# Front state and residual sum turned in 32x32 blocks by VectorE through a DRAM scratch

## The chip, the cores and the metric

One core of one Trainium2 chip. The time is that of the device, in microseconds, from the start to the end of one execution; lower is better. The kernel before takes 1272.34 us, the median of 3 runs (1271.83 to 1272.41).

## What is computed

`x` is 32 graphs of 256 nodes with 256 features, `adj` a sparse 256x256 matrix shared by all. Four layers, each `x = layernorm(x + L(x))`:

```python
# L0: gated graph network, three steps
a = concat(adj @ h, adj @ h)
z = sigmoid(a @ w3.T + h @ u3.T + b);  r = sigmoid(a @ w4.T + h @ u3.T + b)
hv = tanh(a @ w5.T + (r * h) @ u5.T + b);  h = (1 - z) * h + z * hv
# L1: attention without softmax
rel = adj.T * (q @ k.T);  rel = rel / norm(rel, axis=2);  out = rel @ v
# L2: (adj @ x) @ weight + bias
# L3: (D^-1/2 adj D^-1/2) @ (x @ weight) + bias
```

## The kernel before

Everything is fp32. A product is made of three TensorE products of fp32r parts: each operand is split into `hi` (a ScalarE copy that rounds) and `lo` (VectorE: the value minus `hi`). So every tensor that enters a product passes ScalarE and VectorE once. TensorE's products all go through `product` (L430).

Graphs are taken in pairs (16 pairs; two graphs are 512 columns). There are two lanes with their own PSUM banks `ps0` and `ps1`: `front` does steps 1 and 2 of the gated network for pair p, `back` does step 3 for pair q = p - 1 and then, as `main`, the attention and the two convolutions of that pair. One call of `body(p, q)` does all of this; it is written once for each engine as a list in program order, and it runs 14 times (once alone, then 13 times in a `Fori` loop). `finish` does the last pairs in its own order. Semaphores alone order the engines; each engine keeps its list's order, so an operation that waits holds up all behind it on its engine.

One step of a lane is `mix` (adj times h), `base`, `reset`, `update`, `candidate_mixed`, `candidate_reset` on TensorE, each twice (k = 0, 1), with `a_hi`, `reset_gate`, `rh_hi`, `update_gate`, `candidate` on ScalarE and `a_lo`, `reset_h`, `rh_lo`, `keep`, `candidate_part` and the new state (`first_h`, `hand_over_h`) on VectorE. The state is held with features on partitions (`feat`); `mix` of the next step needs it with nodes on partitions (`node_hi`, `node_lo`). `turn_h` (L529) makes that with 4 TensorE transposes a graph into `front.ps1`, from which ScalarE and VectorE make `node_hi` and `node_lo`.

`new_sum` makes the residual sum `sum_t`, again with features on partitions. `turn_sum` (L533) turns it with 4 transposes a graph into `back.ps1`, and from there VectorE takes the statistics (`stats_of`, L1251) and the normalised value (`normalise`, L1267). The products `keys`, `relate` and `values` work on the raw sum, with centred weights; so the relation has to be scaled by 1 / variance, and `mask` (L1307) multiplies by it and by adj in one operation for each half. `values` writes the bank in which the turned sum lay, so it waits for `normalise`. GpSimd makes `rstd` (L362, L364), `inv_var` and `std`; `relation_squares` (L907) scales by `std`.

The input of a pair comes twice: `x_front` in rows, and `x_blocks` in an order in which 32x32 block transposes on VectorE (`turn_blocks`, L1233) give the turned input. SP's queue, in a pass: `load_front`, `load_blocks` (four transfers), `keep_input` (a copy of the turned input for the residual), `store`.

## Time and profile before

| | |
|---|---|
| median of 3 runs | 1272.34 us |
| the profiled execution | 1271.8 us |
| its span, first to last instruction | 1270.0 us |
| TensorE busy | 1240.6 us (98%) |
| VectorE busy | 1031.4 us (81%) |
| ScalarE busy | 583.7 us (46%) |
| GpSimd busy | 192.4 us (15%) |
| mean granted TensorE clock | 0.995 of full |

The profile gives each engine's instructions with start and duration. Busy time is what instructions cover; for TensorE the shown ends of neighbours overlap, so the distance from start to start tells what one costs. An instruction's line is often that of a helper (all products have L430), and the names on it (`f_ps<-hf_feat_hi,u3T_hi`) tell which it is: `f_` is the front lane, `b_` the back lane, `hf_` and `hb_` their states. In lines after "idle before" a releaser is named when the engine stood still.

### The profile page before, as it was taken

What the parts mean: (1) busy time and instruction counts of PE and PEld (TensorE: products, weight loads), DVE (VectorE), ACT (ScalarE), POOL (GpSimd) and SP (SyncE); (2) the same over time, 40 slices, a digit from 0 to 9 for tenths busy, and PEclk for the clock granted to TensorE, in tenths of its full rate; (3) what the DMA queues carried; (4) which work ended last, traced back from release to release, by engine and by line L of the source; (5) the groups of instructions that cost most, each with busy time, mean ns of one, the idle gap of its engine ahead of it and who ended that gap; (6) DMA issues with size and microseconds to landing.
All of it is one profiled execution on the core that took longest, in us unless ns stands there. A gap on an engine that the chain in (4) does not pass through costs nothing.

```text
span 1270.0 us, 21112 instructions
## 1 busy us (share of the span) xinstructions
PE 1240.6 (98%) x7664; PEld 1103.3 (87%) x7664; DVE 1031.4 (81%) x2274; ACT 583.7 (46%) x1007; POOL 192.4 (15%) x366
## 2 busy tenths in 40 slices
PE   7799999999999999999999999999999999999996
PEld 6589899898988989899898988989889898998895
DVE  5668889788888878888788888878888788895898
ACT  4444444444444444454444444444454445444442
POOL 0001112020210202112020110202112021110023
PEclk9999999999999999999999999999999999999999
DMA  7020110202001020010202002020010202000000
GB/s 199 1 50 1 38 30 1 66 0 59 7 17 50 0 66 0 33 33 0 66 0 50 17 17 50 0 66 0 21 45 0 66 0 49 17 17 18 1 1 34
DMA packets 86168, 37.56 MB, mean 30 GB/s; under 512 B 64768, under 2 KB 83200, under 8 KB 86144
## 3 DMA queue, kind: packets, MB, share of 16 engines
q1 hardware_dynamic: 84592, 36.71, 10.6%
q0 software_dynamic: 192, 0.52, 0.2%
q8 instruction: 15, 0.25, 0.1%
q10 hardware_dynamic: 1360, 0.01, 0.1%
q14 instruction: 9, 0.07, 0.0%
HBM read 20.45 MB, written 8.39 MB: 23 GB/s over the span
## 4 chain that ended last, share of the span: by engine, by line
PE 94%; DVE 4%; DMA 1%; POOL 1%; issue 0%; ACT 0%; ACTq 0%; DVEq 0%
PE b_ps L430 46%; PE f_ps L430 43%; PE f_ps L525 2%; PE b_ps L525 1%; DMA bias_in<-in_L_gnn_u_b 1%; PE b_ps L571 1%; DVE f_stats L1251 0%; DVE hf_feat L1267 0%; DVE normed L1267 0%; POOL f_rstd L364 0%; DVE f_cand L1184 0%; DVE b_stats L1251 0%; DVE f_kept L1178 0%; ACTq L827 0%; DVE f_a_lo L1162 0%
## 5 line engine op out<-in xcount | busy, mean ns | idle before, releaser
L362 POOL TENSOR_TENSOR b_var_eps<-b_moments,eps 128x2 f32<-128x2 f32 x120 | 44.1, 368 | 827.6 <-DVE b_moments L1258 827.6
L364 POOL TENSOR_TENSOR b_rstd<-b_var_eps,neg_half 128x2 f32<-128x2 f32 x120 | 97.0, 808 | 9.4
L866 ACT ACTIVATE f_z<-f_ps,bias_z 128x512 f32<-128x512 f32 x66 | 45.2, 685 | 92.5 <-PE f_ps L430 92.5
L870 ACT ACTIVATE f_cand<-f_ps,bias_c 128x512 f32<-128x512 f32 x66 | 45.5, 690 | 85.1 <-PE f_ps L430 85.1
L1168 DVE TENSOR_TENSOR f_gate<-f_gate,hf_feat 128x512 f32<-128x512 f32 x66 | 45.2, 685 | 46.2 <-ACT f_gate L858 46.0
L1251 DVE BATCH_NORM_STATS2 b_stats<-b_ps 128x6 f32<-128x256 f32 x180 | 68.3, 421 | 13.9 <-PE b_ps L430 13.3
L430 PE MATMUL f_ps<-adjT_hi,hf_node_hi 128*128 128x256 f32 x264 | 74.6, 283 | 0.0
L430 PE MATMUL f_ps<-adjT_hi,hf_node_lo 128*128 128x256 f32 x264 | 74.3, 282 | 0.0
L430 PE MATMUL f_ps<-adjT_lo,hf_node_hi 128*128 128x256 f32 x264 | 74.2, 281 | 0.0
L1290 DVE TENSOR_TENSOR b_rh_lo<-b_ps,b_rh_hi 128x512 fp32r<-128x512 f32 x90 | 61.9, 688 | 13.7 <-ACT b_rh_hi L824 13.4
L824 ACT ACTIVATE f_a_hi<-f_ps 128x512 fp32r<-128x512 f32 x66 | 39.0, 593 | 71.8 <-PE f_ps L430 71.8
L824 ACT ACTIVATE b_rh_hi<-b_ps 128x512 fp32r<-128x512 f32 x90 | 53.7, 597 | 34.8 <-PE b_ps L430 32.8
L824 ACT ACTIVATE b_a_hi<-normed 128x512 fp32r<-128x512 f32 x60 | 37.7, 628 | 54.8 <-DVE normed L1267 54.8
L1267 DVE TENSOR_SCALAR normed<-b_ps,b_moments,b_rstd 128x256 f32<-128x256 f32 x120 | 59.3, 536 | 0.3 <-POOL b_rstd L364 0.3
L1162 DVE TENSOR_TENSOR f_a_lo<-f_ps,f_a_hi 128x512 fp32r<-128x512 f32 x66 | 45.2, 686 | 13.8 <-ACT f_a_hi L824 13.6
L1168 DVE TENSOR_TENSOR b_gate<-b_gate,hb_feat 128x512 f32<-128x512 f32 x30 | 20.8, 692 | 43.8 <-ACT b_gate L858 42.6
L858 ACT ACTIVATE f_gate<-f_ps,bias_r 128x512 f32<-128x512 f32 x66 | 45.1, 684 | 24.3 <-PE f_ps L430 24.1
L430 PE MATMUL f_ps<-f_a_hi,w4T_hi 128*128 128x512 f32 x132 | 53.6, 406 | 1.0 <-DVE f_a_lo L1162 1.0
L1184 DVE TENSOR_TENSOR f_cand<-f_z,f_cand 128x512 f32<-128x512 f32 x66 | 45.6, 690 | 9.8 <-ACT f_cand L870 9.8
L430 PE MATMUL f_ps<-f_a_hi,w34T_hi 128*128 128x512 f32 x132 | 53.3, 404 | 0.0
L430 PE MATMUL f_ps<-hf_feat_hi,u3T_hi 128*128 128x512 f32 x132 | 52.5, 398 | 0.3 <-DVE hf_feat_lo L1216 0.3
L372 POOL TENSOR_TENSOR b_norm_inv<-b_norm_sq,neg_half 128x2 f32<-128x2 f32 x30 | 26.0, 866 | 176.4 <-DVE b_norm_sq L1321 176.4
(325 smaller groups left out, 4610.5 us busy)
## 6 DMA issues: line engine op xcount, KB each, us to landing
x_front<-in_x SPq DMA_DIRECT2D x16, 512.0 KB, 3.5
x_blocks<-in_x SPq DMA_DIRECT2D x60, 128.0 KB, 3.4
input_t<-hf_feat SPq DMA_DIRECT2D x15, 512.0 KB, 2.9
out<-result SPq DMA_DIRECT2D x15, 512.0 KB, 3.0
b_cand<-in_L_gnn_u_w SPq DMA_DIRECT2D x2, 256.0 KB, 8.9
bias_out<-in_L_gnn_bias POOLq DMA_DIRECT2D x4, 128.0 KB, 6.3
b_z<-in_L_gnn_w_w SPq DMA_DIRECT2D x1, 512.0 KB, 11.4
b_gate<-in_L_gnn_w_w SPq DMA_DIRECT2D x1, 512.0 KB, 12.4
```

Source lines behind the costliest of these rows:

```text
L364: pool.tensor_tensor(Y.rstd[:, g], Y.var_eps[:, g], neg_half[:], ALU.pow).then_inc(Y.s_rstd, 1)
L430: last = pe.matmul(bank, s, m, start=start and i == 0, stop=stop and i == len(terms) - 1, skip_group_check=True)
L824: return act.activation(dst, src, ACT.Copy)
L858: act.activation(L.gate[:, k], L.ps0[:, k], ACT.Sigmoid, bias=bias_r[:, k:k + 1]).then_inc(L.s_r, 1)
L866: act.activation(L.z[:, k], L.ps0[:, k], ACT.Sigmoid, bias=bias_z[:, k:k + 1]).then_inc(L.s_z, 1)
L870: act.activation(L.cand[:, k], L.ps1[:, k], ACT.Tanh, bias=bias_c[:, k:k + 1]).then_inc(L.s_tanh, 1)
L1162: dve.tensor_tensor(L.a_lo[:, k], L.ps1[:, k], full(L.a_hi[:, k]), ALU.subtract).then_inc(L.s_a_lo, 1)
L1168: dve.tensor_tensor(L.gate[:, k], L.gate[:, k], L.state.feat[:, k], ALU.mult).then_inc(L.s_rh, 1)
L1184: dve.tensor_tensor(L.cand[:, k], L.z[:, k], L.cand[:, k], ALU.mult).then_inc(L.s_zc, 1)
L1251: last = dve.bn_stats(Y.stats[:, g, c], layer_sum(Y, j, g, c))
L1267: last = dve.tensor_scalar(dst[:, g, c], layer_sum(Y, j, g, c), Y.moments[:, g, c, 0:1], Y.rstd[:, g, c:c + 1], ALU.subtract, ALU.mult)
L1290: dve.tensor_tensor(lo[:, g], src, full(hi[:, g]), ALU.subtract).then_inc(done, 1)
```

## The change

In the 14 passes of `body`, the front state after step 1 and the residual sum are no longer turned by TensorE. VectorE transposes 32x32 blocks (`turn_state`, `turn_sum_blocks`, two operations of 128x512 each) into a free SBUF tile, with the four row blocks side by side; SP writes the tile to a DRAM scratch (512 KB) and, when it has landed, reads it back in four transfers of 128 KB, which set the blocks on their final partitions. `moved_hi` and `moved_lo`, `stats_of` and `normalise` read the tile that comes back, in runs of 32 elements. `finish` and the state handed to the back lane keep the TensorE turn.

1 / variance is applied to the values (`values_hi`, `values_lo`) and no more in `mask`, which becomes one operation; `relation_squares` scales by `rstd`, and `std` is gone. `values` waits for `normalise` in `finish` only. The lists of `body` are put in a new order on TensorE, ScalarE, VectorE and GpSimd. The tiles that hold the blocks before and after the trip are tiles of the kernel that are free at the time: `front.gate` and `front.z` for the state, `normed` and `result` for the sum.

```diff
+def scratch(name):
+    return nc.dram_tensor(name, (4, 32, 4, 256), F32).ap()
+
+def quarters(t):
+    return t[:].rearrange("p c (u n) -> p (c u) n", u=2)
+
+state_f.scratch = scratch("turn_f")
+state_f.blocks, state_f.moved = quarters(front.gate), quarters(front.z)
+
...
+main.scratch = scratch("turn_sum")
+main.sum_blocks, main.sum_moved = (t[:].rearrange("p g c d -> p (g c) d") for t in (main.normed, main.result))
...
+    def move_blocks(S, turn):
+
+        sp.wait_ge(S.s_blocks, 2 * turn)
+        sp.dma_start(S.scratch.rearrange("b i a n -> (b i) a n"), S.blocks).then_inc(S.s_written, 16)
+        sp.wait_ge(S.s_written, 16 * turn)
+        for a in range(4):
+            sp.dma_start(S.moved[32 * a:32 * a + 32],
+                         S.scratch[:, :, a].rearrange("b i n -> i b n")).then_inc(S.s_moved, 16)
+
+    def move_sum(Y, q):
+
+        sp.wait_ge(Y.s_sum_blocks, upto(q))
+        sp.dma_start(Y.scratch.rearrange("b i a n -> (b i) a n"), Y.sum_blocks).then_inc(Y.s_sum_written, 16)
+        sp.wait_ge(Y.s_sum_written, 16 * q + 16)
+        for a in range(4):
+            sp.dma_start(Y.sum_moved[32 * a:32 * a + 32],
+                         Y.scratch[:, :, a].rearrange("b i n -> i b n")).then_inc(Y.s_sum_moved, 16)
+
...
         keep_input(p)
+        move_sum(main, p - 1)
+        move_blocks(state_f, p)
         store(main, p - 1)
...
         if j == 0:
             pool.wait_ge(Y.s_rstd, ln(q, 0, g))
             pool.tensor_tensor(Y.inv_var[:, g], Y.rstd[:, g], Y.rstd[:, g], ALU.mult).then_inc(Y.s_inv_var, 1)
-            pool.tensor_tensor(Y.std[:, g], Y.var_eps[:, g], Y.rstd[:, g], ALU.mult).then_inc(Y.s_std, 1)
...
-    def values(Y, q, g):
+    def values(Y, q, g, turned=False):
         pe.wait_ge(Y.s_sum_lo, upto(q))
-        pe.wait_ge(Y.s_normed, ln(q, 0, g))
+        if turned:
+            pe.wait_ge(Y.s_normed, ln(q, 0, g))
...
+    def moved_hi(S, v, g, turn):
+        act.wait_ge(S.s_moved, 64 * turn)
+        if S is state_b and later(v):
+            act.wait_ge(back.s_mixed, upto(v - 1))
+        rows = S.moved[:, :, g * P:(g + 1) * P].rearrange("p q (u i) -> p u q i", i=32)
+        copy(S.node_hi[:, g].rearrange("p h (c q i) -> p (h c) q i", q=4, i=32), rows).then_inc(S.s_node_hi, 1)
+
...
     def values_hi(Y, q, g):
-        graph_hi(Y.v_hi, Y.ps1[:, g], Y.s_v, upto(q, g), g, Y.s_v_hi)
+        act.wait_ge(Y.s_v, upto(q, g))
+        act.wait_ge(Y.s_inv_var, upto(q, g))
+        for c in range(C):
+            last = act.activation(Y.v_hi[:, g, c], Y.ps1[:, g, c * D:(c + 1) * D], ACT.Copy,
+                                  scale=Y.inv_var[:, g, c:c + 1])
+        last.then_inc(Y.s_v_hi, 1)
...
     def relation_squares(Y, q, g):
         act.wait_ge(Y.s_masked, upto(q, g))
-        act.wait_ge(Y.s_std, upto(q, g))
+        act.wait_ge(Y.s_rstd, ln(q, 0, g))
         for c in range(C):
-            last = act.activation(Y.rel_sq[:, g, c], Y.rel[:, g, c], ACT.Square, scale=Y.std[:, g, c:c + 1])
+            last = act.activation(Y.rel_sq[:, g, c], Y.rel[:, g, c], ACT.Square, scale=Y.rstd[:, g, c:c + 1])
         last.then_inc(Y.s_rel_sq, 1)
...
+    def turn_state(S, v, c):
+        dve.wait_ge(S.s_feat, upto(v, c))
+        out = S.blocks.rearrange("p q (u c i) -> p u q c i", c=C, i=32)[:, :, :, c]
+        dve.transpose(out, S.feat[:, c].rearrange("p (u q i) -> p u q i", q=4, i=32)).then_inc(S.s_blocks, 1)
+
+    def moved_lo(S, v, g):
+        dve.wait_ge(S.s_node_hi, upto(v, g))
+        rows = S.moved[:, :, g * P:(g + 1) * P].rearrange("p q (u i) -> p u q i", i=32)
+
+        def cells(t):
+            return t[:, g].rearrange("p h (c q i) -> p (h c) q i", q=4, i=32)
+
+        dve.tensor_tensor(cells(S.node_lo), rows, full(cells(S.node_hi)), ALU.subtract).then_inc(S.s_node_lo, 1)
+
...
+
+    def turn_sum_blocks(Y, q, c):
+        dve.wait_ge(Y.s_sum_t, upto(q, c))
+        if later(q):
+            dve.wait_ge(s_stored, 16 * q)
+        out = Y.sum_blocks.rearrange("p q (u c i) -> p u q c i", c=C, i=32)[:, :, :, c]
+        dve.transpose(out, Y.sum_t[:, c].rearrange("p (u q i) -> p u q i", q=4, i=32)).then_inc(Y.s_sum_blocks, 1)
+
+    def moved_rows(Y, g, c):
+        at = 64 * (C * g + c)
+        return Y.sum_moved[:, :, at:at + 64]

     def layer_sum(Y, j, g, c):
         if j == 1:
             return Y.normed[:, g, c]
...
-    def stats_of(Y, q, j, g):
-        if j == 0:
-            dve.wait_ge(Y.s_sum_turned, upto(q, g))
+    def stats_of(Y, q, j, g, turned=False):
+        if j == 0 and turned:
+            dve.wait_ge(Y.s_sum_turned, g + 1)
+        elif j == 0:
+            dve.wait_ge(Y.s_sum_moved, 64 * q + 64)
...
         for c in range(C):
-            last = dve.bn_stats(Y.stats[:, g, c], layer_sum(Y, j, g, c))
+            src = layer_sum(Y, j, g, c) if j or turned else moved_rows(Y, g, c)
+            last = dve.bn_stats(Y.stats[:, g, c], src)
...
             dve.wait_ge(s_stored, 16 * q)
         for c in range(C):
-            last = dve.tensor_scalar(dst[:, g, c], layer_sum(Y, j, g, c), Y.moments[:, g, c, 0:1],
-                                     Y.rstd[:, g, c:c + 1], ALU.subtract, ALU.mult)
+            src, cells = layer_sum(Y, j, g, c), dst[:, g, c]
+            if j == 0 and not turned:
+                src = moved_rows(Y, g, c).rearrange("p b (h i) -> p h b i", i=32)
+                cells = cells.rearrange("p (h b i) -> p h b i", b=4, i=32)
+            last = dve.tensor_scalar(cells, src, Y.moments[:, g, c, 0:1], Y.rstd[:, g, c:c + 1],
+                                     ALU.subtract, ALU.mult)
         last.then_inc(Y.s_normed, 1)
...
     def values_lo(Y, q, g):
-        graph_lo(Y.v_lo, Y.v_hi, graph_bank(Y.ps1, g), Y.s_v_hi, upto(q, g), g, Y.s_v_lo)
+        dve.wait_ge(Y.s_v_hi, upto(q, g))
+        for c in range(C):
+            last = dve.scalar_tensor_tensor(Y.v_lo[:, g, c], Y.ps1[:, g, c * D:(c + 1) * D],
+                                            Y.inv_var[:, g, c:c + 1], full(Y.v_hi[:, g, c]), ALU.mult,
+                                            ALU.subtract)
+        last.then_inc(Y.s_v_lo, 1)

     def mask(Y, q, g):

         dve.wait_ge(Y.s_rel, upto(q, g))
-        dve.wait_ge(Y.s_inv_var, upto(q, g))
-        for c in range(C):
-            last = dve.scalar_tensor_tensor(Y.rel[:, g, c], Y.ps0[:, g, c * N:(c + 1) * N],
-                                            Y.inv_var[:, g, c:c + 1], adj_nat[:, c], ALU.mult, ALU.mult)
-        last.then_inc(Y.s_masked, 1)
+        dve.tensor_tensor(Y.rel[:, g], graph_bank(Y.ps0, g), adj_nat[:], ALU.mult).then_inc(Y.s_masked, 1)

...
```

TensorE's new list in `body` (P = 2p, N = 2p+1; the last number is k or g):

```
mix(back) 0,1; base(back) 0,1; mix(front,P) 0; reset(back) 0,1; update(back) 0,1; candidate_mixed(back) 0;
candidate_reset(back) 0; candidate_mixed(back) 1; candidate_reset(back) 1; mix(front,P) 1; base(front,P) 0,1;
reset(front,P) 0,1; update(front,P) 0,1; candidate_mixed(front,P) 0; candidate_reset(front,P) 0;
candidate_mixed(front,P) 1; candidate_reset(front,P) 1; keys 0,1; values 0; relate 0; values 1; relate 1;
base(front,N) 0; sum_squares 0; base(front,N) 1; attend 0; mix(front,N) 0,1; sum_squares 1; attend 1;
reset(front,N) 0,1; candidate_mixed(front,N) 0; mix_nodes 0,0; update(front,N) 0; mix_nodes 0,1;
convolve 0,0; convolve 0,1; update(front,N) 1; candidate_reset(front,N) 0; candidate_mixed(front,N) 1;
candidate_reset(front,N) 1; mix_nodes 1,0; mix_nodes 1,1; turn_h(state_b) 0,1; convolve 1,0; convolve 1,1
```

VectorE's new list in `body` (P = 2p, N = 2p+1; the second number is k or g; of `main`'s, j comes before it):

```
input_nodes_lo 0,1; a_lo(back) 0,1; turn_blocks 0; reset_h(back) 0; input_lo 0; reset_h(back) 1; rh_lo(back) 0;
a_lo(front,P) 0; rh_lo(back) 1; keep(back) 0; residual 0; keep(back) 1; turn_blocks 1; candidate_part(back) 0;
input_lo 1; residual 1; new_sum 0; candidate_part(back) 1; turn_sum_blocks 0; new_sum 1; a_lo(front,P) 1;
turn_sum_blocks 1; reset_h(front,P) 0; sum_lo 0; reset_h(front,P) 1; rh_lo(front,P) 0,1; keep(front,P) 0,1;
sum_lo 1; stats_of 0,0; stats_of 0,1; candidate_part(front,P) 0; first_h 0; turn_state 0;
candidate_part(front,P) 1; first_h 1; turn_state 1; moments_of 0,0; keys_lo 0,1; feat_lo(state_f,N) 0;
moments_of 0,1; normalise 0,0; mask 0; normalise 0,1; feat_lo(state_f,N) 1; values_lo 0; mask 1;
squares_sum 0; relation_lo 0; norms 0; values_lo 1; moved_lo 0,1; sum_attended 0; squares_sum 1;
stats_of 1,0; relation_lo 1; moments_of 1,0; a_lo(front,N) 0; norms 1; a_lo(front,N) 1; normalise 1,0;
sum_attended 1; stats_of 1,1; moments_of 1,1; fill 0,0; conv_x_lo 0,0; normalise 1,1; reset_h(front,N) 0;
fill 0,1; conv_x_lo 0,1; conv_ax_lo 0,0; reset_h(front,N) 1; keep(front,N) 0; rh_lo(front,N) 0; conv_ax_lo 0,1;
stats_of 2,0; moments_of 2,0; rh_lo(front,N) 1; stats_of 2,1; normalise 2,0; moments_of 2,1; fill 1,0;
conv_x_lo 1,0; keep(front,N) 1; normalise 2,1; candidate_part(front,N) 0; fill 1,1; hand_over_h 0;
conv_x_lo 1,1; candidate_part(front,N) 1; hand_over_h 1; conv_ax_lo 1,0; (the rest as before)
```

ScalarE's list follows the same order: `input_nodes_hi` first, `update_gate(back)` between the two `rh_hi(back)`, and around the state turn `candidate(front, 2p)` 0,1; `feat_hi` 0; `keys_hi` 0,1; `values_hi` 0; `feat_hi` 1; `relation_squares` 0; `values_hi` 1; `relation_hi` 0; `moved_hi` 0,1; `relation_hi` 1; `relation_squares` 1; `a_hi` 0,1.

## Rows read from the trace of the kernel before

**Rows 1.** The page's part on busy time: share of the span and count of each engine.
```profile
PE 1240.6 (98%) x7664; PEld 1103.3 (87%) x7664; DVE 1031.4 (81%) x2274; ACT 583.7 (46%) x1007; POOL 192.4 (15%) x366
```

**Rows 2.** Windows: start:end and length, each engine's busy us, clock, DMA share, GB/s.
```profile
447.22:523.72 76.50, 76.50 (x479) 68.25 (x478) 63.55 (x140) 35.78 (x62) 11.91 (x22) 1.00 0.10 27
...
70.70:1141.50 1070.80, 1070.80 (x6666) 955.45 (x6665) 890.49 (x1962) 501.44 (x870) 166.80 (x308) 1.00 0.10 27
1190.00:1270.00 80.00, 66.52 (x490) 61.73 (x488) 70.02 (x192) 28.32 (x50) 21.75 (x44) 0.96 0.04 14
```

**Rows 3.** Timeline of TensorE: start, duration, instruction. First matmuls of successive blocks.
```profile
406.63 0.39 PE L430 MATMUL f_ps<-f_a_hi,w5T_hi 128*128 128x512 f32 x1
...
408.03 0.40 PE L430 MATMUL f_ps<-f_rh_hi,u5T_hi 128*128 128x512 f32 x1
...
410.84 0.28 PE L430 MATMUL b_ps<-b_rh_hi,sum_hi 128*128 128x256 f32 x1
```

**Rows 4.** Timeline of TensorE: a state turn, and one graph of the sum turn.
```profile
412.26 1.04 PE L525 MATMUL f_ps<-ident,hf_feat 128*128 128x128 f32 x8
413.05 0.36 PE L430 MATMUL b_ps<-wvT_hi,sum_hi 128*128 128x256 f32 x1
413.25 0.28 PE L430 MATMUL b_ps<-wvT_lo,sum_hi 128*128 128x256 f32 x1
413.37 0.28 PE L430 MATMUL b_ps<-wvT_hi,sum_lo 128*128 128x256 f32 x1
...
471.02 0.60 PE L525 MATMUL b_ps<-ident,b_cand 128*128 128x128 f32 x4
471.38 0.48 PE L430 MATMUL f_ps<-f_a_hi,w4T_hi 128*128 128x512 f32 x1
471.69 0.39 PE L430 MATMUL f_ps<-f_a_lo,w4T_hi 128*128 128x512 f32 x1
```

**Rows 5.** Groups of VectorE: busy us, mean ns of one, idle before.
```profile
L1307 DVE SCALAR_TENSOR_TENSOR b_gate<-b_ps,b_inv_var,adj_nat 128x256 f32<-128x256 f32 x60 | 26.2, 478 | 0.1
L1233 DVE STREAM_TRANSPOSE hf_feat<-x_blocks 128x512 f32<-128x512 f32 x30 | 21.0, 704 | 0.0
L1290 DVE TENSOR_TENSOR v_lo<-b_ps,v_hi 128x512 fp32r<-128x512 f32 x30 | 20.6, 687 | 3.9 <-ACT v_hi L824 3.9
```

**Rows 6.** Timeline of ScalarE.
```profile
411.04 0.60 ACT L824 ACTIVATE v_hi<-b_ps 128x512 fp32r<-128x512 f32 x1 [0.72 <-PE b_ps L430]
...
454.41 0.69 ACT L858 ACTIVATE b_gate<-b_ps,bias_r 128x512 f32<-128x512 f32 x1 [3.60 <-PE b_ps L430]
```

**Rows 7.** Timeline of VectorE; the last of the three needs the one before it.
```profile
409.71 0.69 DVE L1178 SCALAR_TENSOR_TENSOR f_kept<-f_z,hf_feat 128x512 f32<-128x512 f32 x1
410.35 0.69 DVE L1184 TENSOR_TENSOR f_cand<-f_z,f_cand 128x512 f32<-128x512 f32 x1
411.17 0.69 DVE L1190 TENSOR_TENSOR hf_feat<-f_cand,f_kept 128x512 f32<-128x512 f32 x1
```

**Rows 8.** Timeline of GpSimd: from the moments to `rstd`.
```profile
423.73 0.55 POOL L362 TENSOR_TENSOR b_var_eps<-b_moments,eps 128x2 f32<-128x2 f32 x1 [3.11 <-DVE b_moments L1258]
424.36 1.02 POOL L364 TENSOR_TENSOR b_rstd<-b_var_eps,neg_half 128x2 f32<-128x2 f32 x1
```

**Rows 9.** SP's queue: issues of a pass in the timeline; sizes and landings; `x_blocks` landings in the loop.
```profile
451.20 0.40 SPq L334 DMA_DIRECT2D out<-result  x1
...
462.39 3.10 SPq L316 DMA_DIRECT2D x_blocks<-in_x  x4
468.61 0.54 SPq L324 DMA_DIRECT2D input_t<-hf_feat  x1
...
x_front<-in_x SPq DMA_DIRECT2D x16, 512.0 KB, 3.5
...
out<-result SPq DMA_DIRECT2D x15, 512.0 KB, 3.0
...
DMA to landing us min/median/max: 2.9/3.4/3.8
```

More of the change, by code:

```diff
@@ L961, in body @@
                 conv_ax_hi(main, q, 0, 0)
[L962 to L963 removed]
+                reset_gate(front, 2 * p + 1, 1)
+                update_gate(front, 2 * p + 1, 0)
                 rh_hi(front, 2 * p + 1, 0)
```

243 lines of the change are left out of this document (122 added, 121 removed).

## The prediction

> **What bounds the kernel now.** I read the busy shares first: TensorE is busy 98% of the span [rows 1]. That is an average, so I read it by stretch next. In the stretch of the 14 passes of `body` TensorE is busy 1070.80 of 1070.80 us at the full granted clock (1.00, the 2.4 GHz level), and one pass from its first matmul (`mix(back, q, 0)`) to that of the next is 76.50 us with no idle time at all, while VectorE is busy 63.55 and ScalarE 35.78 of it [rows 2]. So in the loop time falls only if TensorE's own list gets shorter, and an edit costs something only if it makes TensorE wait. The last 80 us are different: TensorE 66.52, VectorE 70.02 [rows 2]. Durations on a saturated TensorE I take from start to start, since the shown ends overlap: a block of six 128x512 matmuls takes 1.40 us (406.63 to 408.03), one of twelve 128x256 takes 1.42 us (410.84 to 412.26) [rows 3, 4].
>
> **What goes.** `turn_sum` (2 x 4 transposes) and `turn_h(state_f, ...)` (8) leave the pass; `turn_h(state_b, ...)` and everything in `finish` stay. The eight of one state turn run from 412.26 to 413.05, and the first matmul behind them takes 0.20 to the next start where its like takes 0.12: 0.79 + 0.08 = 0.87 us. Four of the sum run 471.02 to 471.38, and the next matmul takes 0.31 in place of 0.23: 0.44, twice 0.88 [rows 4]. Together 1.75 us a pass, 24.5 us in 14 passes, if nothing waits. The arithmetic left is 52 blocks of 1.40 to 1.42, one state turn and two `sum_squares`; the pass would be 76.50 - 1.75 = 74.75.
>
> **What comes on VectorE.** Four 128x512 block transposes a pass, 0.70 each in the rows, here with an output in runs of 32 elements, which no row shows: between nothing extra and double [rows 5]. I take 0.70, as the operation is the same. Reading rows of 32 elements in `moved_lo`, `moved_hi`, statistics and normalisation is likewise unseen; I take the plain price. `mask` turns from two operations of 0.48 into one of about 0.69, and `values_lo` from one of 0.69 into two of about 0.48 [rows 5]: they cancel. VectorE comes to about 63.55 + 2.8 = 66.4 of 74.75, so it isn't the bound by its sum, only by its order. ScalarE's `values_hi` becomes two operations (about 0.9 in place of 0.60 [rows 6]), GpSimd loses `std`; both have room.
>
> **The order, walked.** Since TensorE never waits now, each block's start is the sum of those ahead of it. I call the first matmul of `mix(back, q, 0)` 0 and take 1.40 or 1.41 a block. VectorE starts an operation of 128x512 some 0.60 to 0.64 after the one before, an operation on its own last result starts 0.82 after, and one lasts 0.69 [rows 7]; ScalarE starts some 0.06 after TensorE and lasts 0.60 to 0.69 [rows 6]; moments to `rstd` on GpSimd I take at 1.2, where one shown took 1.65 [rows 8]. The points where the new lists are tight:
> - First part: `a_lo(back)` ends at 6.1, its user starts at 7.0; the gate of `update(back, 1)` is there at 10.6 for 11.2; `rh_lo` at 13.3 for 14.0; `a_lo(front, 2p, 1)` at 21.5 for 22.4. No wait. `mix(front, 2p, 0)`, moved to 5.6, has its nodes at 4.9.
> - The sum turn: `turn_sum_blocks` ends at 22.1. Its only reader in line is `stats_of(main, q, 0, 0)`, which VectorE reaches at 30.1. Behind it are `candidate_part(front, 2p, 0)`, not due before 31.6, `first_h` and `turn_state`; the pair of statistics takes 1.4, so a landing by 30.2 costs nothing, a budget of 8.1 us, and up to 0.5 more is absorbed before `candidate_part(..., 1)` at 34.4. `values` no longer waits for the normalisation.
> - The state turn: `turn_state(..., 1)` ends at 36.8. `mix(front, 2p+1, 0)` starts at 46.7 and needs both `moved_lo`. After the landing two `moved_hi` and the second `moved_lo` take about 1.9, so a landing by 44.7 is free: a budget of 7.9 us. Behind `moved_hi` on ScalarE stand `relation_hi(1)` and `relation_squares(1)`, due about 0.4 later than that.
> - Between: `feat_lo(1)` at 41.4 for `base` at 42.1; `squares_sum(0)` at 43.2 for 43.5; `relation_lo(1)` at 49.3 for 49.9; `a_lo(front, 2p+1, 1)` at 50.9 for 51.3. Room of 0.3 to 0.7 each.
> - Tail: `conv_ax_lo(0, 1)` ends at 61.15 for `convolve(0, 1)` at 61.17, since only one block now stands between it and `mix_nodes(0, 1)`: a wait of up to 0.1. The convolution layers now start about 3 us nearer the end of the pass, and VectorE is late there: `conv_x_lo(1, 1)` ends at 69.8 for `mix_nodes(1, 1)` at 69.6: a wait of 0.2.
> So about 0.3 us of new waits a pass stands on this walk, with an error of the same size.
>
> **The round trip.** On SP's queue, per turn: a 512 KB write to DRAM, a wait, four 128 KB reads. Write: 3.0, that of the output store, the same size to the same memory. Reads: their issue steps bounded by 0.40 (a store's issue) and 0.84 (four `x_blocks` issues take 3.10 in all, the last 0.58), three steps; the last lands after 2.9 (the lowest of `x_blocks`, also 128 KB, but in 128-byte pieces) to 3.5 (`x_front`, four times the bytes in pieces of 1 KB) [rows 9]. With 0.1 for the wait: 3.0 + 0.1 + 1.2 + 2.9 = 7.2 at the low end, 3.0 + 0.1 + 2.5 + 3.5 = 9.1 at the high end. I take steps of 0.54, the issue of `input_t`, whose addresses also need no register work, and 2.9: 7.6. That is under both budgets, by 0.3 for the state. SP isn't held up otherwise: `x_blocks` is issued from 15.7, `input_t` at about 18.8, both before the sum is turned at 22.1; `store` comes last as before.
>
> At the store row 512 KB take 3.0 us. The Trainium skill, page "DMA: Bandwidth & Descriptors", section "Anatomy of one DMA — SWDGE (gpsimd) path", gives about 2.0 us fixed plus bytes over 436e3; that would be 3.2 for the write and 2.3 for a read, and the round trip 7.2 with the same steps, an estimate from that page. By it the waits would be those of the walk alone and the time that of my forecast.
>
> **The sum.** 14 x (1.75 - 0.30) = 20.3 us. The profiled execution is 1271.8 us (span 1270.0 and 1.8 around it), so it gives 1251.5; from the median of 1272.34 it gives 1252.0. `finish` I cost at nothing: `mask` and `values_lo` cancel, and the second half of `values_hi` (0.3 us, four times) stands beside other work; without that cover it costs 1.2.
>
> **The rivals.**
> - A, the forecast: small waits, 0.1 to 0.5 a pass: 1249.6 to 1255. Chance 0.50.
> - B, no wait at all: 14 x 1.75 = 24.5: 1247.8. For it: my walk rounds every hand-over up. Chance 0.10.
> - C, the round trip sticks out in part, or a strided transpose takes double. At 9.1 us `mix(front, 2p+1, 0)` waits 9.1 - 7.9 = 1.2, with the walk's 0.3 a gain of 0.25 a pass: 3.5, or 1268.8; at 8.5 us it is 1260. A second transpose of 1.4 takes 0.7 from the budget: wait 0.4, time 1258. Chance 0.25, of which 0.04 within 0.2% of before.
> - D, slower: the round trip to the state decides. Its break-even is 7.9 + 1.75 - 0.3 = 9.4 us. No row shows reads right behind a write to the same DRAM rows; if for that they land in 5 instead of 2.9, the trip is 9.7 at my steps and 10.6 at the long ones. At 10.6 the pass gets 2.7 + 0.3 - 1.75 = 1.25 longer: 17.5 us, 1290. Against it: `x_blocks` lands within 2.9 to 3.8 in all of the loop [rows 9]. Chance 0.12.
> - E, the blocks are turned, but TensorE's time doesn't fall, because transposes fill room that the matmuls behind them would leave anyway. Then 1272. Against it: the blocks of 1.40 beside them are not shorter for having no turn before them [rows 3]. Chance 0.03.
>
> A transpose costs 0.11 on TensorE in the rows, and a turn through VectorE costs 1.4 us of VectorE and 7.6 of latency. The Trainium skill, page "VectorE: DVE Perf Modes", section "Rules for kernel authors", says to transpose 128x128 with TensorE if PSUM will do, and speaks against this change; if its reason held here, D would be its result, and I give it no more than D has, since TensorE is the bound [rows 2].
>
> **How the numbers follow.** Chances: A 0.50, B 0.10, C 0.25, D 0.12, E 0.03. Predicted is A's 1252.0. The range holds A, B and most of C and leaves out D and the upper edge of C: 1247 to 1267. A difference of 0.2% (2.5 us) is about what a measurement of this kernel can tell from none. Faster by more: A, B and 0.21 of C: 0.81. Within: 0.04 of C, 0.03 of E: 0.07. Slower: 0.12.
>
> **What the profile after should show.** The pass at 75.0 us (74.75 to 75.3) on TensorE; 14 x 16 = 224 fewer transposes, 136 - 112 = 24 of `hf_feat` left; SP's second read group landed 7.2 to 8.2 us after the second `turn_state`; no wait of TensorE for `moved_lo`, and short ones for `conv_x_lo` and `conv_ax_lo`; VectorE about 66 us a pass. Wrong would be: TensorE waiting for `hf_node_lo` for over 0.5 us a pass (C or D), a block transpose over 1 us (C), or a VectorE wait for the sum's landing that pushes `keys_lo` past 37.9.

## The result and the profile after

| | before | after |
|---|---|---|
| median | 1272.38 us (1271.83 to 1273.25, 4 runs) | 1262.12 us (1261.86 to 1263.57, 4 runs) |
| ratio | | 0.9921 (0.9904 to 0.9938) |
| span of the profiled execution | 1270.0 us | 1260.2 us |
| a pass of `body` on TensorE | 76.50 us | 75.64 us |

The change gains 10.3 us. The prediction was 1252.0, a gain of 20.3: the sign is right and the time lies inside the range, but half of the gain isn't there. So there are two questions: where the other half went, and what holds it.

The page's part on busy time, of the kernel after, answers [rows 1]:

```profile
span 1260.2 us, 20942 instructions
...
PE 1226.0 (97%) x7440; PEld 1082.3 (86%) x7440; DVE 1058.8 (84%) x2330; ACT 591.5 (47%) x1039; POOL 185.3 (15%) x334
```

TensorE has 224 instructions less, 16 a pass, as the change says, and is busy 14.6 us less; but its span fell by only 9.8. VectorE has 27 us more. The windows answer [rows 2]: one pass, the stretch in it where the convolutions stand, and the 13 passes of the loop (columns: start:end and length; busy us and instructions of TensorE, its weight loads, VectorE, ScalarE, GpSimd; clock; DMA share; GB/s).

```profile
444.86:520.50 75.64, 75.34 (x462) 66.66 (x461) 65.51 (x146) 36.27 (x64) 11.45 (x20) 1.00 0.19 55
506.40:524.20 17.80, 17.54 (x120) 16.12 (x121) 17.18 (x44) 8.55 (x15) 4.62 (x8) 1.00 0.00 0
142.27:1125.62 983.35, 979.48 (x5982) 866.83 (x5981) 851.43 (x1874) 471.02 (x831) 148.93 (x260) 1.00 0.19 56
```

TensorE now stands idle 0.30 us in a pass, where [rows 2] had none, at the same full clock. The second line is what to look at: VectorE is busy 65.51 of 75.64 in the pass, but 17.18 of 17.80 in its last part. The mean of the pass hides a stretch in which VectorE has almost no room. The kernel before is close to that too. This is its window over the same work, from the first statistics of the first convolution layer to `base(back, 0)`:

```profile
508.07:526.51 18.44, 18.44 (x126) 16.89 (x126) 17.04 (x44) 7.73 (x13) 4.58 (x8) 1.00 0.00 0
```

There VectorE is busy 17.04 of 18.44, so 1.40 us were free; now 0.62 are.

**Where the 9.8 us of span come from.** 13 passes by 76.50 - 75.64 = 0.86 give 11.2. What follows the 14th pass takes 134.58 instead of 134.29, so `finish` costs 0.3 more. And the second pass begins at 142.27 instead of 141.22, 1.05 later, where the first pass should have brought it 0.86 earlier: 1.9 are lost there. 0.92 of that lie ahead of the first pass, which begins at 64.27 instead of 63.35, and 0.79 in its first block (4.96 us instead of 4.17). TensorE has the same work up to there in both kernels; what differs is the clock that it was granted (in the first block 0.59 on the mean of 64.00 to 70.00, where before has 0.82). The window in which this shows best, in before and then in after:

```profile
38.20:42.00 3.80, 3.77 (x20) 3.23 (x21) 2.97 (x6) 1.40 (x3) 0.00 (x0) 1.00 0.00 0
```

```profile
38.20:42.00 3.80, 3.74 (x10) 2.99 (x11) 3.00 (x7) 1.43 (x3) 0.00 (x0) 0.56 0.00 0
```

In the same list, 20 matmuls fit at 1.00 (the 2.4 GHz level) and 10 at a mean of 0.56, near the lower level of 1.2 GHz; in the 4.20 us ahead of it TensorE had been busy 1.34 us in before and 1.37 in after, at a clock of 1.00 and 0.99. In the kernels below the second pass begins anywhere from 142.6 to 144.1 (146.9 in the one with the longer state trip, 159.5 in the old order with both trips), 1 / variance alone at 142.63 and the old order with fewer transposes at 143.86, though both have the lists of before. The kernel before alone took from 1270.96 to 1274.19 us in 19 runs. So I put the 1.9 us down to scatter of the clock ahead of the loop, without having tested it, and compare by the pass.

**Where the pass loses.** The prediction wants 74.75 without a wait. I lay the first matmuls of successive blocks side by side, as in [rows 3], and look for pairs of blocks longer than 24 x 0.118 = 2.83 us. Two stand out; `convolve(1, ...)` takes 2.88, but it took 2.89 in before. This is TensorE's timeline at both (start, duration, instruction):

```profile
504.80 0.28 PE L463 MATMUL b_ps<-w2s_hi,b_rh_hi 128*128 128x256 f32 x1
...
506.09 0.27 PE L463 MATMUL b_ps<-w2s_hi,b_rh_lo 128*128 128x256 f32 x1
506.48 0.36 PE L463 MATMUL b_ps<-w2s_hi,b_rh_hi 128*128 128x256 f32 x1
...
507.95 0.40 PE L463 MATMUL f_ps<-f_a_hi,w34T_hi 128*128 128x512 f32 x1
...
513.56 0.28 PE L463 MATMUL b_ps<-norm_adjT_hi,b_a_hi 128*128 128x256 f32 x1
...
514.85 0.27 PE L463 MATMUL b_ps<-norm_adjT_hi,b_a_lo 128*128 128x256 f32 x1
515.31 0.38 PE L463 MATMUL b_ps<-norm_adjT_hi,b_a_hi 128*128 128x256 f32 x1 [0.19 <-DVE b_a_lo L1365]
```

`convolve(0, 0)` and `(0, 1)` take 507.95 - 504.80 = 3.15, so 0.32 is lost, at the step from 506.09 to 506.48. No wait is written there, because the shown end of the matmul before hides most of it: the gap has to be read from start to start. `mix_nodes(1, ...)` takes 3.26, so 0.43 is lost, of which the line names 0.19. Together 0.75; 74.75 + 0.75 = 75.50, and about 0.1 is spread over other blocks. So nearly all of the loss lies at two steps, and little is left for a cost of the added memory traffic that shows nowhere. These are the two waits that the prediction named (0.1 and 0.2), each larger by a bit over 0.2.

VectorE at these places. The first line is the last operand of `convolve(0, 1)`, the one at 514.57 that of the second `mix_nodes(1, ...)`; the group from 513.37 shows how an operation of 128x512 starts every 0.60 with nothing between. The last line is `normalise(3, 0)` in the next pass, which `base(back, 0)` waits for.

```profile
505.64 0.69 DVE L1365 TENSOR_TENSOR b_rh_lo<-b_ps,b_rh_hi 128x512 fp32r<-128x512 f32 x1
...
508.15 0.76 DVE L1322 BATCH_NORM_STATS2 b_stats<-b_ps 128x6 f32<-128x256 f32 x2
508.88 1.00 DVE L1342 TENSOR_SCALAR normed<-b_ps,b_moments,b_rstd 128x256 f32<-128x256 f32 x2
...
513.37 0.69 DVE L1360 TENSOR_TENSOR b_ps<-normed,bias_out 128x512 f32<-128x512 f32 x1
513.97 0.68 DVE L1232 TENSOR_TENSOR hb_feat<-f_cand,f_kept 128x512 f32<-128x512 f32 x1
514.57 0.68 DVE L1365 TENSOR_TENSOR b_a_lo<-normed,b_a_hi 128x512 fp32r<-128x512 f32 x1
...
522.14 0.96 DVE L1342 TENSOR_SCALAR result<-b_ps,b_moments,b_rstd 128x256 f32<-128x256 f32 x2
```

`b_rh_lo` ends at 506.33 and its matmul starts at 506.48. `b_a_lo` ends at 515.25 and its matmul starts at 515.31, 0.34 after its turn came at 514.97.

**The round trips.** SP's queue in a pass (issues), and the page's lines on DMAs (count, KB each, median us from issue to landing), which answer [rows 9]:

```profile
467.12 0.35 SPq L358 DMA_DIRECT2D turn_sum<-normed  x1
469.75 1.74 SPq L361 DMA_DIRECT2D result<-turn_sum  x4
481.68 0.34 SPq L349 DMA_DIRECT2D turn_f<-f_gate  x1
484.36 1.73 SPq L352 DMA_DIRECT2D f_z<-turn_f  x4
```

```profile
turn_sum<-normed SPq DMA_DIRECT2D x14, 512.0 KB, 2.6
...
result<-turn_sum SPq DMA_DIRECT2D x56, 128.0 KB, 2.9
...
turn_f<-f_gate SPq DMA_DIRECT2D x14, 512.0 KB, 2.7
...
f_z<-turn_f SPq DMA_DIRECT2D x56, 128.0 KB, 2.9
```

And who takes the state up, ScalarE and then VectorE, with the second `turn_state` of that pass ahead of them:

```profile
480.94 0.71 DVE L1270 STREAM_TRANSPOSE f_gate<-hf_feat 128x512 f32<-128x512 f32 x1
...
488.72 1.15 ACT L854 ACTIVATE hf_node_hi<-f_z 128x512 fp32r<-128x512 f32 x2 [1.43 <-DMA f_z<-turn_f]
...
489.82 1.28 DVE L1279 TENSOR_TENSOR hf_node_lo<-f_z,hf_node_hi 128x512 fp32r<-128x512 f32 x2
```

From the end of the transpose (481.65) to ScalarE's start the trip takes 7.07 us: 2.68 from issue to issue, three steps of 0.43, 2.9 and the hand-overs. `mix(front, 2p+1, 0)` starts at 491.70, and `hf_node_lo` is done at 491.10. TensorE waits for neither trip; for the state's, `hf_node_lo` has 0.6 to spare.

### The profile page after: what moved, and what is told of

Its sections match the earlier page's. It is cut to its first block, busy times and chain, and to the rows that moved or that the text cites. A ratio compares the mean times of both kernels' runs of the same rounds, so it can differ in the third digit from the quotient of the medians.

```text
span 1260.2 us, 20942 instructions
## 1 busy us (share of the span) xinstructions
PE 1226.0 (97%) x7440; PEld 1082.3 (86%) x7440; DVE 1058.8 (84%) x2330; ACT 591.5 (47%) x1039; POOL 185.3 (15%) x334
## 4 chain that ended last, share of the span: by engine, by line
PE 86%; DVE 10%; issue 1%; DMA 1%; POOL 1%; ACT 0%; ACTq 0%; DVEq 0%
PE b_ps L463 45%; PE f_ps L463 38%; DVE normed L1342 2%; DVE b_a_lo L1365 1%; PE f_ps L558 1%; DVE b_stats L1322 1%; DMA bias_in<-in_L_gnn_u_b 1%; DVE f_kept L1220 1%; PE b_ps L605 1%; DVE f_cand L1226 1%; DVE b_ps L1360 1%; DVE hb_feat L1232 1%; DVE hf_feat L1342 0%; POOL f_rstd L398 0%; DVE f_stats L1322 0%
## 5 line engine op out<-in xcount | busy, mean ns | idle before, releaser
L396 POOL TENSOR_TENSOR b_var_eps<-b_moments,eps 128x2 f32<-128x2 f32 x120 | 40.2, 335 | 939.9 <-DVE b_moments L1329 939.9
L900 ACT ACTIVATE f_cand<-f_ps,bias_c 128x512 f32<-128x512 f32 x66 | 45.3, 687 | 76.6 <-PE f_ps L463 76.6
L463 PE MATMUL f_ps<-hf_feat_lo,u3T_hi 128*128 128x512 f32 x132 | 52.7, 399 | 0.0
L463 PE MATMUL f_ps<-hf_feat_hi,u3T_lo 128*128 128x512 f32 x132 | 52.5, 397 | 0.0
L463 PE MATMUL f_ps<-f_rh_lo,u5T_hi 128*128 128x512 f32 x132 | 52.2, 396 | 0.0
L463 PE MATMUL f_ps<-f_rh_hi,u5T_lo 128*128 128x512 f32 x132 | 52.2, 396 | 0.0
L463 PE MATMUL f_ps<-f_a_hi,w5T_hi 128*128 128x512 f32 x132 | 52.2, 396 | 0.0
```

What stands on the lines that cost most here:

```text
L396: pool.tensor_tensor(Y.var_eps[:, g], Y.moments[:, g, :, 1], eps[:], ALU.add).then_inc(Y.s_var, 1)
L463: last = pe.matmul(bank, s, m, start=start and i == 0, stop=stop and i == len(terms) - 1, skip_group_check=True)
L900: act.activation(L.cand[:, k], L.ps1[:, k], ACT.Tanh, bias=bias_c[:, k:k + 1]).then_inc(L.s_tanh, 1)
```

## The experiments

Each ran beside the kernel before on the same chip, in three groups (medians of before 1273.15, 1273.38 and 1272.85). The theory: TensorE's gross gain of 1.75 us is there, and what takes 0.89 of it back is the new order: it puts attention 2.5 us later in the pass (`attend(1)` ends at 51.5 of the pass instead of 49.0), to cover the state's trip, so that the convolutions and all of VectorE's work behind them must fit in a shorter rest of the pass. Rivals: a transpose gives TensorE less than its price in the rows; the trips or the memory traffic cost something that isn't seen as a wait; 1 / variance costs; a plain mistake in the order of a few operations.

### The price of the transposes

The sum's transposes are put back in one piece, unused; all else as after.

```diff
+for k in range(2): turn_unused(main, q, k)      # turn(Y.ps1, g, Y.sum_t, ...), ahead of keys
 for k in range(2):
     keys(main, q, k)
```

> The kernel after, with the 8 transposes of the sum a pass put back on TensorE ahead of keys, into the bank that values writes later; nobody reads them. Theory 'gross gain as in the rows': they cost 0.88 us a pass, 12.3 us in 14, so about 1274.4. Rival 'a transpose on TensorE costs less than the rows say, so there was less to gain': 1262 to 1268.

1273.57 us (1272.63 to 1274.78), ratio 1.0004 (0.9995 to 1.0014). The passes take 76.51 on the mean (142.64 to 678.22 for seven), which is 0.87 more than after. Eight transposes cost 0.87; the prediction has 0.88 for the sum's. The time went to 1273.6 where 1274.4 was expected. So the gross gain is real, and rival E falls: a transpose doesn't fill room that would be there anyway.

### 1 / variance alone

The kernel before with `values_hi`, `values_lo`, `relation_squares` and `mask` as in after; order and turns as before.

```diff
-act: copy(v_hi, ps1)                       dve: v_lo = ps1 - v_hi;  rel = ps0 * inv_var * adj
+act: v_hi = ps1 * inv_var (each half)      dve: v_lo = ps1 * inv_var - v_hi (each half);  rel = ps0 * adj
```

> The kernel before, with only the part that moves 1/variance from the mask to the values (and rstd in place of std in relation_squares); order and turns as before. Theory: TensorE has no idle time in the passes and both turns of cost on VectorE cancel, so 1271.5 to 1273.5. Rival 'this part costs': values_hi as two operations makes attend or sum_squares late, 0.2 us a pass or more, 1275 or above; that would be the missing gain.

1273.27 us (1271.86 to 1274.5), ratio 1.0004 (0.9994 to 1.0014), the pass 76.50 as in before. It costs nothing and gives nothing by itself, as taken in the sum: in after the `v_lo` pair takes 0.87 on VectorE and `mask` 0.69.

### The round trip: how much room the cover leaves

Two kernels, one for the state and one for the sum: in each the write to its scratch is issued twice, the second when the first has landed, so that the trip is longer by 2.7 us. This is the edit for the state.

```diff
 sp.dma_start(S.scratch..., S.blocks).then_inc(S.s_written, 16)
-sp.wait_ge(S.s_written, 16 * turn)
+sp.wait_ge(S.s_written, 32 * turn - 16)
+sp.dma_start(S.scratch..., S.blocks).then_inc(S.s_written, 16)
+sp.wait_ge(S.s_written, 32 * turn)
```

> The kernel after, with the write of the state's blocks to the scratch done twice, one after the other, which makes that round trip 2.7 us longer. Theory: the trip of 7.05 us stands against a budget of 8.0, so 2.7 more sticks out by 1.75 us a pass at mix(front, 2p+1, 0): about 1262 + 24.5 = 1286.5 (1283 to 1291). Rival 'the trip is hidden deeper, since other waits absorb it': under 1275. Rival 'the trip already sticks out today': 2.7 a pass or more, 1300.

> The kernel after, with the write of the sum's blocks done twice in a row (2.7 us more on that round trip). Its landing moves from about 474.0 to 476.7 in the pass shown, where VectorE reaches the statistics at 475.06. Theory: VectorE waits 1.6 us there, of which the waits behind it absorb some; keys_lo(0), with 0.2 us of room, comes 0.8 late for relate(0): 0.5 to 0.7 us a pass, 1268 to 1273. Rival 'budget of 8.1 plus 0.5 as in the prediction, the rest 1:1': trip 6.9 + 2.7 = 9.6 against 8.6, 1.0 a pass, 1276. Rival 'hidden': 1262.

With the state's write doubled: 1292.16 us (1290.13 to 1292.39), ratio 1.0151 (1.0134 to 1.0168). The waits of TensorE between 100 and 1120 us (what waits, for what: us in total, times, longest):

```profile
PE f_ps L465 <- DVE hf_node_lo L1281: 22.6, 13, 3.6
PE b_ps L465 <- DVE b_a_lo L1367: 2.4, 13, 0.2
```

`mix(front, 2p+1, 0)` now waits 1.73 a pass, where 1.75 was expected, and the pass takes 77.44, 1.8 more than after. The time is above the 1283 to 1291 expected, because the first pass loses more than the others: it waits 3.6, since the first trip is longer (8.2 instead of 7.07 in after itself), and the second pass begins at 146.89, 4.6 later than in after. This is the prediction's rival D made on purpose: with 2.7 us more, the change is slower than the kernel before.

With the sum's write doubled: 1277.12 us (1275.78 to 1278.26), ratio 1.0031 (1.0019 to 1.0043). VectorE:

```profile
482.53 1.41 DVE L1324 BATCH_NORM_STATS2 b_stats<-result 128x6 f32<-128x256 f32 x4 [1.65 <-DMA result<-turn_sum]
```

and the waits of TensorE:

```profile
PE b_ps L465 <- DVE b_rh_lo L1367: 11.0, 14, 1.8
PE b_ps L465 <- DVE b_a_lo L1367: 2.4, 13, 0.2
```

VectorE stands at `stats_of` for 1.65, and with it all that is queued behind: `first_h`, `turn_state`, and `keys_lo` (`b_rh_lo`), for which `relate(0)` waits. The place is the one predicted ("a VectorE wait for the sum's landing that pushes `keys_lo`"); the price, 1277 for an expected 1268 to 1273, is larger, and nearer to the rival's 1276, by which what exceeds the prediction's budget is lost one to one: the passes take 76.6 on the mean of 13 (143.43 to 1139.54), 1.0 more than after, of which the wait of 11.0 / 14 = 0.8 is the shown part. So the sum's trip too has less than 2.7 us of room, but at its real length it costs nothing: `stats_of` starts at 475.06 in after, with no wait.

### The turns in the old order

The new turns, with the lists of `body` in the order of before.

```diff
 (TensorE)  ... values 0; relate 1; -turn_h(state_f) 0,1-; values 1; sum_squares 0; attend 0; ...
 (VectorE)  ... new_sum 0,1; +turn_sum_blocks 0,1+; sum_lo; stats_of 0,0 ...; first_h; +turn_state 0,1+ ...
```

> Both turns through the scratch and 1/variance on the values, but all lists of body in the order of the kernel before (turn_sum_blocks around new_sum, turn_state behind first_h, moved_hi and moved_lo where node_hi and node_lo stood). Theory 'the new order is what hides the trips': the statistics wait about 4 us for the sum with reset_h and rh_lo of the front lane queued behind them, and mix(front, 2p+1, 0) waits about 5 us for the state: 6 to 9 us a pass, 1340 to 1390. Rival 'the order does little, the trips fit anyway': 1248 to 1265.

1470.71 us (1468.52 to 1472.91), ratio 1.1551 (1.1525 to 1.1576). Dearer than expected: a pass takes 90 to 91 instead of 76.5. The window of one pass:

```profile
522.93:612.97 90.04, 78.94 (x463) 69.12 (x461) 65.30 (x144) 36.07 (x64) 11.61 (x20) 0.96 0.16 47
```

the two longest waits of TensorE, and VectorE where the sum's turn comes back:

```profile
PE f_ps L463 <- DVE hf_node_lo L1279: 57.8, 11, 6.3
PE b_ps L463 <- DVE sum_lo L1369: 52.2, 12, 4.5
```

```profile
546.12 0.71 DVE L1300 STREAM_TRANSPOSE normed<-b_cand 128x512 f32<-128x512 f32 x1
...
554.09 0.75 DVE L1322 BATCH_NORM_STATS2 b_stats<-result 128x6 f32<-128x256 f32 x2 [5.07 <-DMA result<-turn_sum]
554.76 0.67 DVE L1369 TENSOR_TENSOR sum_lo<-b_cand,sum_hi 128x512 fp32r<-128x512 f32 x1
```

TensorE waits 57.8 / 11 = 5.3 us at a time for `hf_node_lo`, the trip of the state laid bare, and 52.2 / 12 = 4.4 for `sum_lo`, which doesn't need the trip at all: it is queued on VectorE behind `stats_of`, which does. In the window TensorE is idle for 90.04 - 78.94 = 11.1. It is also busy 4.2 longer than the 74.75 of its list, at a mean clock of 0.96 where after has 1.00: with waits like these part of the loop runs below the 2.4 GHz level. My expectation of 1340 to 1390 had 6 to 9 us of waits and nothing for the clock. So the new order is what makes the change pay. What takes 1.75 - 0.86 = 0.89 of the gain back is the question of the runs that follow.

### Is it the order of a few operations?

`fill(1, 1)` goes behind `conv_ax_lo(1, 0)` and `feat_lo(state_b, 0)` behind `conv_ax_lo(1, 1)`, which makes the operand of the second wait 0.6 earlier.

```diff
-fill(main, q, 1, 1)
 hand_over_h(p, 0)
 conv_x_lo(main, q, 1, 1)
 candidate_part(front, 2 * p + 1, 1)
 hand_over_h(p, 1)
 conv_ax_lo(main, q, 1, 0)
-feat_lo(state_b, p, 0)
+fill(main, q, 1, 1)
 conv_ax_lo(main, q, 1, 1)
+feat_lo(state_b, p, 0)
```

> The kernel after, with VectorE's fill(1,1) moved behind conv_ax_lo(1,0), and feat_lo(state_b,0) behind conv_ax_lo(1,1). Theory 'late VectorE tail': of the 0.9 us a pass that the change fell short of its 1.75, 0.44 is TensorE waiting at mix_nodes(1,1) for conv_x_lo(1,1), because VectorE runs without a gap there and fill(1,1), not due before convolve(1,1), stands ahead of it. Then this wait vanishes, the pass goes from 75.64 to 75.2 and the time to about 1256. Rival 'the wait moves on' (to turn_h(state_b) or convolve(1,1)): 1259 to 1262. Rival 'the shortfall is contention by the added DMA traffic': no change, 1262.

1261.93 us (1261.53 to 1263.15), ratio 0.9912 (0.9896 to 0.9929), the pass 75.63: no gain over after. The wait at `mix_nodes(1, ...)` is gone (2.88 instead of 3.26), and the same time is missing at the start of the next pass. VectorE's last operation ahead of it, and TensorE:

```profile
523.33 0.96 DVE L1342 TENSOR_SCALAR result<-b_ps,b_moments,b_rstd 128x256 f32<-128x256 f32 x2
```

```profile
523.98 0.28 PE L463 MATMUL b_ps<-adjT_hi,hb_node_lo 128*128 128x256 f32 x1
524.35 0.50 PE L463 MATMUL b_ps<-hb_feat_hi,u3T_hi 128*128 128x512 f32 x1
```

`base(back, 0)` writes the bank that `normalise(3, 0)` reads. Its turn comes at 524.10, `normalise` ends at 524.29, and it starts at 524.35; in all 0.24 to 0.35 a pass is lost there. VectorE goes without a gap from 509.30 (`stats_of(2, 1)`) to 524.3. My own expectation was 1256, and it failed; the rival that the wait moves on (1259 to 1262) came true. I had taken the wait as one of order, and it is one of load. A chain of operations that has no gap only hands its delay to the next reader.

The starts from end to end say how much is missing. From the end of `convolve(0, 1)` to `base(back, 0)` TensorE's blocks take 16.28 in before (510.23 to 526.51, no wait). In the new order one block of 1.40 less stands there: 14.88 without a wait. VectorE's chain over the same stretch holds it to 509.10 to 524.35 in this kernel, 15.25. The 0.37 between is lost in every pass, at whichever reader the order puts it.

### Is it VectorE's load in that stretch?

As in the last kernel, and the two `feat_lo(state_b, ...)` of a pass do 64 of 512 columns; the other columns keep stale values.

```diff
-feat_lo(state_b, p, k)         # 128x512
+feat_lo_part(state_b, p, k)    # 128x64
```

> The kernel of e1_fill_late, where both feat_lo(state_b, k) of a pass, still on VectorE, compute only 64 of their 512 columns (the low part of the back lane's state is left stale in the rest): about 0.9 us less VectorE work between the end of convolve(0,1) and base(back,0), no work on another engine. Theory 'VectorE's work in that stretch is the bound': the wait of e1 at base(back,0) goes, the pass falls from 75.63 to 75.2, the time to about 1256 to 1257. Rival 'the wait at base is the latency through statistics, GpSimd and normalisation': no change, 1262.

1256.26 us (1255.02 to 1257.64), ratio 0.9867 (0.9849 to 0.9885), inside what was expected. The pass falls to 75.26, the wait at the pass's start is gone, and `convolve(0, 1)` keeps its 0.34. VectorE:

```profile
517.08 0.21 DVE L1263 TENSOR_TENSOR hb_feat_lo<-hb_feat,hb_feat_hi 128x64 fp32r<-128x64 f32 x1
...
520.06 0.21 DVE L1263 TENSOR_TENSOR hb_feat_lo<-hb_feat,hb_feat_hi 128x64 fp32r<-128x64 f32 x1
```

A `feat_lo` starts its successor after 0.60 in the kernel before this one and after 0.13 here, so 2 x 0.47 = 0.94 us of VectorE's work are gone from the stretch. Some 0.35 of that was needed: the pass falls by 0.37. That separates the causes: the second loss (0.43) is VectorE's load behind `convolve(0, 1)`, and the first (0.32) is something else, since it stays.

### Is the first loss the hand-over, and does it matter?

`update(front, 2p+1, 1)`, one block of 1.4 us, goes between `convolve(0, 0)` and `convolve(0, 1)`.

```diff
-for k in range(2):
-    convolve(main, q, 0, k)
+convolve(main, q, 0, 0)
 update(front, 2 * p + 1, 1)
+convolve(main, q, 0, 1)
```

> The kernel after, with TensorE's update(front, 2p+1, 1) moved in between the two convolve(0, k), so that 2.8 us stand between mix_nodes(0,1) and its use in convolve(0,1) instead of 1.4. Theory 'VectorE full in the last third': the chain mix_nodes, conv_ax_hi, conv_ax_lo, convolve takes 1.68 us from block end to block start, so this wait of 0.33 goes, but VectorE has no gap from there to the end of the pass and gets convolve(0,1) 1.1 us later, so the waits behind grow by as much or more: 1262 to 1268. Rival 'two independent short waits': the 0.33 is gained, 14 x 0.33 = 4.6: 1257.5.

1275.92 us (1274.83 to 1276.68), ratio 1.0021 (1.0011 to 1.0030), well above the 1262 to 1268 expected: slower than after, as the theory said, but by far more. The wait at `convolve(0, 1)` is gone, and 1.78 instead of 0.43 is lost at `mix_nodes(1, ...)`. VectorE, and then the waits of TensorE:

```profile
514.38 0.76 DVE L1322 BATCH_NORM_STATS2 b_stats<-b_ps 128x6 f32<-128x256 f32 x2 [1.18 <-PE b_ps L463]
```

```profile
PE b_ps L463 <- DVE b_a_lo L1365: 19.9, 13, 1.5
```

`stats_of(2, 1)` starts when `convolve(0, 1)` has ended. With a block put before it, that end comes 1.40 - 0.32 = 1.08 later, VectorE stands idle for 1.18, and `mix_nodes(1, ...)`, which for want of the first wait is due 0.32 earlier, finds its operand 1.08 + 0.32 = 1.40 later than it did; 1.35 more are lost there. So the stretch has a start as well as a length: it begins at the end of `convolve(0, 1)`, and what that comes later is lost one to one.

### Another engine for a part of the load

`feat_lo(state_b, ...)` on GpSimd, otherwise as the kernel with the late `fill`.

```diff
-dve: feat_lo(state_b, p, k)
+pool: feat_lo(state_b, p, k)      # behind inverse_std(2, ...)
```

> The kernel of e1_fill_late, with both feat_lo(state_b, k) of a pass on GpSimd, ahead of its inverse_std(3, k): 1.2 us of VectorE's work at the end of the pass gone, nothing else changed. Theory 'VectorE full in the last third': then VectorE is 1.2 us earlier at the normalisation for which base(back) waited in e1, the wait of 0.4 vanishes and the pass falls from 75.63 to about 75.25, if GpSimd takes under 2 us for one: 1256 to 1258. Rival 'what waits there is the chain through GpSimd's rstd or ScalarE, not VectorE's sum': no change, 1262. Rival 'GpSimd is slow or in VectorE's way': 1264 or above.

1268.21 us (1267.45 to 1270.17), ratio 0.9959 (0.9945 to 0.9973), the pass 76.1: worse than after, and not the 1256 to 1258 of the theory but what the third possibility, GpSimd slow or in VectorE's way, put at 1264 or above. GpSimd takes 1.44 us on the mean, and it isn't only slow. The groups by line (busy us, mean ns of one, idle before), first of this kernel and then of the one it is made from:

```profile
L409 POOL TENSOR_TENSOR hb_feat_lo<-hb_feat,hb_feat_hi 128x512 fp32r<-128x512 f32 x28 | 40.3, 1439 | 86.9 <-ACT hb_feat_hi L861 86.9
...
L1239 DVE TENSOR_TENSOR hb_feat<-f_cand,f_kept 128x512 f32<-128x512 f32 x30 | 33.0, 1100 | 3.9
```

```profile
L1232 DVE TENSOR_TENSOR hb_feat<-f_cand,f_kept 128x512 f32<-128x512 f32 x30 | 20.8, 693 | 3.9
```

In one pass, GpSimd and then the VectorE operation that starts while it runs:

```profile
518.85 1.57 POOL L409 TENSOR_TENSOR hb_feat_lo<-hb_feat,hb_feat_hi 128x512 fp32r<-128x512 f32 x1 [3.23 <-ACT hb_feat_hi L861]
```

```profile
519.41 1.57 DVE L1239 TENSOR_TENSOR hb_feat<-f_cand,f_kept 128x512 f32<-128x512 f32 x1
```

This VectorE operation, which reads two SBUF tiles, lasts 1.57 instead of 0.69 and ends at 520.98; `turn_h(state_b, ...)`, which needs it, starts at 521.03, 0.84 late. It happens once in each pass, so the mean of the group goes from 693 to 1100 ns. Beside the other `feat_lo` of the pass (523.41, 1.30) VectorE reads PSUM, and its operations keep their 1.27 and 0.75. Of the 1.2 us that GpSimd takes over, VectorE loses 0.88 again, at a place where TensorE waits for it.

### The same gain without the new order

The kernel before, in its own order, with one transpose instead of four in each of `turn_sum` and `turn_h(state_f, ...)` in `body`; nothing takes their place, so three quarters of the turned data are stale.

```diff
-for c in range(C):
-    for k in range(C):
-        pe.transpose(ps1[...c, k], feat[...k, c], ident)
+pe.transpose(ps1[...1, 1], feat[...1, 1], ident)
```

> The kernel before in its own order, with one transpose in place of four in every turn_sum and turn_h(state_f) of a pass: 12 of 16 left out and nothing put in their place (three quarters of what they turn is stale). Theory 'TensorE's time in the old order falls 1:1, and it is the new order that gives part back': 12 x 0.11 = 1.31 us a pass, 18.4 in all, minus little: 1254 to 1256. Rival 'with a shorter list TensorE runs into VectorE at the end of the pass in any order': the old order has 0.7 us of room there, so up to 0.6 a pass is lost, 1258 to 1263.

1255.74 us (1254.11 to 1257.54), ratio 0.9862 (0.9844 to 0.9879), as expected. The pass is 75.20, which is 76.50 - 1.30, three quarters of 1.75, with no wait of TensorE anywhere in the loop. In the old order TensorE's shortening is passed on one to one, and VectorE follows with 75.20 as the pass. In after, 1.75 are taken out and 0.86 arrive. So 75.64 isn't a floor under the pass. This kernel also leaves out the block transposes and the trips, so alone it doesn't say which part of the change costs the rest. The trace of after does: no block ahead of `convolve(0, 1)` loses more than some hundredths, and both losses stand at steps that the new order made shorter (one block instead of two between `mix_nodes(0, 1)` and `convolve(0, 1)`, and one block less behind it). In the old order the transposes go out ahead of that stretch, and it keeps its 16.28.

No kernel was found that beats after clearly while it does all of the work; the late `fill` equals it.

## Why the prediction was half right

**What bounds the kernel**: right. TensorE did, and the passes still end on it.

**What goes**: right. 1.75 a pass; the sum's part measured alone is 0.87 for a term of 0.88, and three quarters of all gave 1.30.

**What comes on VectorE**: right. A block transpose with its output in runs of 32 takes 0.70 to 0.71, as taken; the range up to double wasn't needed. VectorE's pass is 65.51 for 66.4. `values_hi` takes 0.84 in two operations for 0.9, and 1 / variance costs nothing.

**The round trip**: right, and somewhat too long. 7.07 for 7.6, because the write lands in 2.6 to 2.7 (3.0 taken) and the issue steps are 0.43 (0.54 taken). The four reads right behind a write to the same rows land after 2.9, no later than `x_blocks` (2.9 to 3.8 in [rows 9]); D and C stayed empty. By the Trainium skill's page "DMA: Bandwidth & Descriptors", section "Anatomy of one DMA — SWDGE (gpsimd) path", the write would be 3.2 and a read 2.3, an estimate from its fit; the runs show 2.6 to 2.7 and 2.9, so the page is above the one and below the other, and only their sum comes near.

**The room for the trip**: right. TensorE waits for neither, and the doubled write made it wait 1.73, where the walk's room of 7.9 gives 7.07 + 2.7 - 7.9 = 1.87.

**The order, walked**: this is the step that failed. It found the two places, and it gave 0.1 and 0.2 where the trace has 0.32 and 0.43, with about 0.1 more spread over the pass. The term of the sum was 0.30 and measured 1.75 - 0.86 = 0.89: 14 x 0.59 = 8.3 of the 10.5 us that the span lacks. The reasons:
- Hand-overs. From `mix_nodes(0, 1)` to `convolve(0, 1)` the result passes ScalarE and VectorE while one block of 1.41 runs. This is ScalarE's line for it:

```profile
505.00 0.60 ACT L854 ACTIVATE b_rh_hi<-b_ps 128x512 fp32r<-128x512 f32 x1 [0.20 <-PE b_ps L463]
```

  ScalarE starts 0.20 after the next block's first matmul (504.80), where I took 0.06; the rows had it already, since `v_hi` starts at 411.04 in [rows 6] and the block behind its product at 410.84 in [rows 3]. It lasts 0.60; VectorE starts 0.04 later (0.03 to 0.04 also where it had been idle) and lasts 0.69; TensorE starts 0.15 after that, where I took nothing. In all 1.68 for a cover of 1.41: 0.27, and 0.32 in the trace. I had said that my walk "rounds every hand-over up"; here it rounded them down.
- A delay isn't used up by the reader that waits. The walk compared each result with its reader and stopped there. VectorE's list from `stats_of(2, 1)`, which starts 0.20 behind the end of `convolve(0, 1)`, to the end of `normalise(3, 0)` in the next pass (508.15 to 523.10) has no gap. Everything in it moves with its start, and its length is what a pass must hold; the late `fill`, another order inside it, only moved the wait, and the short `feat_lo`, less load, took it away.
- The shift. The prediction says that the convolutions "now start about 3 us nearer the end of the pass, and VectorE is late there", and then costs this with a single wait. The pass's mean, 66 of 75, says that VectorE has 9 us of room; in this stretch it has 0.6 of 17.8, and before the change it had 1.4 of 18.4.

**The rest of the miss** is 1.9 us ahead of the second pass, beside the lower clock shown above, and 0.3 in `finish`, which I had at nothing: 8.3 + 1.9 + 0.3 = 10.5.

**The rivals.** What happened is A's mechanism with a size outside A's own range of 1249.6 to 1255, and inside what was left for C; but C's mechanism, a trip that sticks out, is not it. B (no wait) and E (no gain) fell. D's break-even is real: 2.7 us more of trip made it 1292.

**Ranges.** A reached to 0.5 us of waits a pass. Hand-overs that were unknown by 0.25 at each of its two tight places ask for 0.3 + 0.5 = 0.8, which is 1272.3 - 14 x 0.95 = 1259 as its upper end.

What the Trainium skill's page "VectorE: DVE Perf Modes" says in "Rules for kernel authors", that a 128x128 transpose belongs on TensorE, isn't borne out by this case: with TensorE as the bound, 0.87 us of its time was worth 1.4 of VectorE's and 7 of latency, as long as the order hid the trip. Without that order, at 1470 us, the page's rule would have been the better advice.

## What to carry to other kernels

When work leaves the engine that bounds a kernel and returns as latency, the price is paid in the order that hides the latency: find what was moved later to make the cover, and walk the stretch behind it for gaps, not only each result against its reader. Read the second engine's share in that stretch and not over the pass (17.18 of 17.80 beside 65.51 of 75.64), and ahead of the change: 17.04 of 18.44 leaves 1.40, just the block that the new order takes out of the stretch, with nothing over for hand-overs. A cheap test ahead of the work is to leave the removed operations out in the old order (76.50 to 75.20 for three quarters of them), which gives the gross gain, and to compare with it what the full change brings.

## What the hardware showed that I had not expected

- A VectorE operation of 128x512 that reads two SBUF tiles and started while a GpSimd one of the same size ran lasted 1.57 us instead of 0.69; operations that read PSUM beside GpSimd kept their time (1.27 and 0.75).
- On its way from TensorE through ScalarE and VectorE back to TensorE, a result of 128x512 took 1.68 us, of which 0.39 are hand-overs (0.20, 0.04, 0.15).
- The four reads right behind a write to the same DRAM rows landed after 2.9, no later than reads without one (2.9 to 3.8). The first trip of an execution is longer: the state's took 8.2 us in after (from 103.22 to 111.38), where the later ones take 7.07.
- The clock granted to TensorE ahead of the loop differs between executions of the same list (1.00 and 0.56 in the same 3.8 us); the start of the second pass lay between 141.2 and 144.1 in the kernels without a state trip laid bare, and in the two that keep the lists of before at 142.63 and 143.86, where before has 141.22.
